# A four-layer graph network on one core: where GpSimd copies the next sixteen gather indices

## The reference, cut to what matters

```python
h = jnp.maximum(_layernorm(x, axis=-1), 0.0)
weight = jnp.einsum('rb,bio->rio', w_comp, bases)     # 32 relations from 8 bases
h_rel = jnp.einsum('ni,rio->rno', h, weight)
msg = h_rel[edge_type_32, src] * edge_weight1
x = x + jax.ops.segment_sum(msg, dst, num_segments=1250) + h_bias
```

## Time and profile before

| | |
|---|---|
| median of 3 runs | 1577.9 us (1575.59 to 1578.49) |
| the profiled execution | 1579.06 us |
| its span in the profile | 1577.2 us |
| TensorE busy in the span | 1462.6 us (93%) |
| VectorE | 993.9 us (63%) |
| ScalarE | 328.9 us (21%) |
| GpSimd | 887.9 us (56%) |
| mean granted TensorE clock | 0.985 of full speed |
| gathers of the first stage (L740) | 36.1 to 449 us of the span |

### The profile page before, as it was taken

The page is one execution under the profiler, slowest core; times in us unless marked ns, Lnnn a source line. Parts: engine busy times, 40 slices in busy tenths (PEclk is TensorE's granted clock), DMA queues, the critical chain, the costliest instruction groups (busy, mean ns, idle before and its releaser), DMA issues.

```text
span 1577.2 us, 24690 instructions
## 1 busy us (share of the span) xinstructions
PE 1462.6 (93%) x6784; PEld 941.4 (60%) x6785; DVE 993.9 (63%) x2781; ACT 328.9 (21%) x806; POOL 887.9 (56%) x932
## 2 busy tenths in 40 slices
PE   4888888888889999999999998999999988999999
PEld 2777777777754444433447576666666655566465
DVE  8766666666666888898633333888888873421111
ACT  7000000000000000000062223555555545411100
POOL 5677777777722777677667761777777760000000
PEclk9999999999999999999999998999999998999999
DMA  4676666776765223422411111322222230000000
GB/s 159 192 198 199 192 203 201 203 202 199 200 173 164 78 74 92 136 83 70 125 61 25 26 28 62 105 72 64 72 65 70 68 54 1 28 0 1 27 34 34
DMA packets 91857, 159.19 MB, mean 101 GB/s; under 512 B 18747, under 2 KB 46960, under 8 KB 91792
## 3 DMA queue, kind: packets, MB, share of 16 engines
q0 software_dynamic: 42832, 103.15, 23.3%
q1 hardware_dynamic: 33728, 29.73, 6.0%
q10 hardware_dynamic: 15232, 25.52, 5.4%
HBM read 140.63 MB, written 17.70 MB: 100 GB/s over the span
## 4 chain that ended last, share of the span: by engine, by line
PE 52%; issue 15%; POOL 14%; DMA 12%; DVE 3%; ACT 1%; POOLq 1%; SPq 1%; DVEq 0%; ACTq 0%
PE ps L1148 14%; PE ps L935 12%; POOL u L801 11%; DMA gath<-h_rows,idx 10%; PE ps L923 9%; PE ps L878 8%; PE ps L1110 4%; POOL gath L740 3%; DMA u<-u_rows,at 2%; PE ps L1129 2%; PE ps L914 1%; PE ps L973 1%; DVE et L1299 0%; PE ps L1085 0%; DMA wc_blk<-in_w_comp_dram 0%
## 5 line engine op out<-in xcount | busy, mean ns | idle before, releaser
L878 PE MATMUL ps<-spread,gath 128*128 128x128 f32 x2504 | 354.9, 290 | 55.1 <-DMA gath<-h_rows,idx 43.8
L766 POOL DMA_INDIRECT slots<-att,idx_s x313 | 313.0, 1000 | 117.2 <-issue 92.9
L878 PEld LDWEIGHTS ps<-spread,gath 128*128 128x128 f32 x2504 | 306.5, 195 | 103.3 <-issue 59.5
L740 POOL DMA_INDIRECT gath<-h_rows,idx x313 | 300.3, 960 | 109.5 <-issue 58.8
L1148 PE MATMUL ps<-base_t,z 128*128 128x512 f32 (+1 forms) x640 | 311.6, 613 | 1.8 <-ACT z L527 1.0
L801 POOL DMA_INDIRECT u<-u_rows,at x243 | 239.1, 984 | 109.7 <-issue 70.7
L1361 DVE TENSOR_TENSOR z<-z,ps 128x512 f32 x313 | 215.0, 687 | 84.1 <-PE ps L878 69.1
L935 PE MATMUL ps<-hs,adj 128*128 128x512 f32 (+3 forms) x400 | 165.5, 414 | 0.0
L1038 PE MATMUL ps<-msg,hot 128*128 128x256 f32 x648 | 158.0, 388 | 6.4 <-DVE msg L1716 5.4
L935 PE MATMUL ps<-hl,adj 128*128 128x512 f32 (+3 forms) x400 | 157.6, 394 | 0.0
L1038 PEld LDWEIGHTS ps<-msg,hot 128*128 128x128 f32 x648 | 120.8, 192 | 56.5 <-DVE msg L1716 36.2
(11 more groups left out here) (264 smaller groups left out, 1678.3 us busy)
## 6 DMA issues: line engine op xcount, KB each, us to landing
base_t<-in_bases_dram ACTq DMA_DIRECT2D x64, 256.0 KB, 2.7
slots<-zero_t SPq DMA_DIRECT2D x6, 896.0 KB, 6.0
at<-slots SPq DMA_DIRECT2D x21, 256.0 KB
att<-in_attr_dram SPq DMA_DIRECT2D x79, 64.0 KB
gath<-h_rows,idx POOLq DMA_INDIRECT x313, 3.7
slots<-att,idx_s POOLq DMA_INDIRECT x313
u<-u_rows,at POOLq DMA_INDIRECT x243, 2.5
z<-in_x_dram SPq DMA_DIRECT2D x9, 256.0 KB, 5.1
```

The costliest lines, as they stand in the source:

```text
L740: nc.gpsimd.indirect_dma_start(out=gath[:, c % RING, :], out_offset=None, in_=h_rows, in_offset=bass.IndirectOffsetOnAxis(ap=idx[:, par, c ...
L766: nc.gpsimd.indirect_dma_start(out=slots, out_offset=bass.IndirectOffsetOnAxis(ap=idx_s[0:r, turn_of, at_quad * QUAD + c:at_quad * QUAD + ...
L878: last = mm(bank[:, k * P:(k + 1) * P], gath[:, h_slot, k * P:(k + 1) * P], s_of.rearrange("p b d -> p (b d)"), start=True, stop=True)
```

## The change

The copy of a lap's indices is no longer the first instruction of the lap. It is issued in the middle of the lap before, between the wait for the slot of gather c = 8 and that gather, into the other half of idx. The copy for the first lap is issued by itself ahead of all gathers. The wait for idx_ok at c = 0 stays, with the same numbers, and so does the count of copies: the last lap of nine gathers issues none. No other engine's program is changed.

```diff
+            def copy_indices(at_chunk, par):
+                nc.gpsimd.tensor_copy(idx[:, par, :], src_i[:, bass.ds(at_chunk, 2 * RING)]).then_inc(idx_ok, 1)
+
             def gather_lap(i, par, first, chunks=2 * RING):
 
                 at_chunk = i * 4 * RING + par * 2 * RING
-                nc.gpsimd.tensor_copy(idx[:, par, :], src_i[:, bass.ds(at_chunk, 2 * RING)]).then_inc(idx_ok, 1)
                 indexed = in_reg(pool, i * 2 + par + 1)
...
                     if c == 0:
                         pool.wait_ge(idx_ok, indexed)
+                    if c == RING and chunks == 2 * RING:
+                        copy_indices(at_chunk + 2 * RING, 1 - par)
                     nc.gpsimd.indirect_dma_start(
...
             with pool.If(pool.value_load(fits[0:1, 0:1], min_val=0, max_val=1) == 1):
+                copy_indices(0, 0)
                 for par in range(2):
                     gather_lap(0, par, par == 0)
```

## The result

| | before | after |
|---|---|---|
| median | 1576.9 us of 4 runs | 1563.5 us of 4 runs (1560.84 to 1566.55) |
| ratio to before | | 0.9907, 95% interval 0.9892 to 0.9923 |
| profiled execution, span | 1579.06, 1577.2 us | 1560.84, 1559.0 us |
| first start of the first to the last gather | 411.95 us | 395.90 us |
| TensorE's mean granted clock | 0.985 | 0.987 |

The kernel is faster by 13.4 us, 0.9%. The forecast was 1574.2 us, and its range ended at 1567: the sign was right, the saving was three to four times what I had put down.

The account below looks back on a forecast made before the run. GpSimd's gathers, one per 1.25 us, were taken to bound the first stage. A gross saving of 10.1 us less 6.4 given back to holds made 3.7, so 1577.9 - 3.7 = 1574.2 us, range 1567 to 1580.

Parts of the forecast that it names:

- TensorE doesn't become the bound: First stage: TensorE has 18.24 us to do in a lap of at least 20.2; its becoming the bound got no chance.
- The hold itself: A gather starting just behind VectorE's spread (L1352) takes longer, by about 0.57 us less the distance between the starts.
- the row that feeds itself: Slower rival, first stage: held gathers sustain themselves, 42 of 75 spreads at 0.43 us, 1582.4 us; chance 0.12.
- the copy's cost behind it: Mid-lap copy: next gather 0.24 us after it, 0.46 from gather to gather, so 0.18 us added a lap.
- the bounds given, 0 to 0.68: Mid-lap copy's cost: 0 if it fits into the 0.30 us between gathers, at most the whole 0.68 of the boundary.
- the gross saving: 19 lap boundaries: 0.71 us removed less 0.18 added by the mid-lap copy, 10.1 us in all.
- the entries: Gathers c = 11 newly caught behind their spread: 5 to 8 of 16, taken as 0.4 of 19 laps.
- The give-back: New holds of gathers by spreads, 9.9 us, less 3.5 us of present extra that goes: 6.4 us net.
- The stall: A gap of 2.19 us between gathers just behind one boundary; a possible further 1.9 us saved, not counted.
- the holds don't grow: Rival: the copy hides in the 0.30 us or the spread comes later; full saving of 10.1 us, 1567.8; chance 0.20.
- The two rivals with more holds: Holds eat the whole saving, 1579.1 us, chance 0.20; or held gathers sustain themselves, 1582.4 us, chance 0.12.
- a gather behind any copy needs 0.78 us: Rival: the gap behind the copy stays, wait or not, so the change saves nothing, 1577.9 us; chance 0.03.

Follow-up runs that it names:

- wait_behind: Changed kernel, but gather c = 8 waits at once for the mid-lap copy ahead of it; 1578.1 us, ratio to the kernel before 0.9996.
- copies2: Changed kernel with the mid-lap index copy cut into two parts, one behind the other; 1575.2 us, ratio to the kernel before 0.9976.
- copies4: Changed kernel with the mid-lap index copy cut into four parts, one behind the other; 1576.8 us, ratio to the kernel before 0.9991.
- copies8_c: Changed kernel with the mid-lap index copy cut into eight parts, one behind the other; 1579.5 us, ratio to the kernel before 1.0008.
- copy_at_15_c: Changed kernel with the next lap's copy between gathers c = 14 and c = 15; 1566.4 us, ratio to the kernel before 0.9919.
- after_again: The changed kernel run once more, unedited; 1566.7 us, ratio to the kernel before 0.9929.

## Why the prediction fell short, point by point

**What held.** GpSimd sets the stage's pace with 1.25 us a gather, and the boundary costs 0.71 us because the queue runs empty behind the wait: the lap fell from 20.72 to 20.11, and wait_behind, which has the copy in its new place and the wait, gave nothing. That TensorE doesn't become the bound held too: 18.24 us of work in 20.11. There are 20 copies, 19 of them between gathers, and no gap of 0.98. The hold itself, a gather caught just behind a spread, with the 0.57 less the distance, is what copies2, copies4 and copies8_c show; the row that feeds itself stands in copy_at_15_c. Two readings of rows were slightly off and bear on nothing: the gap of 0.30 us stands before 289 gathers, not 291, and the four of the earlier trace rows are not the last of the 14 long ones, two come behind them.

**The step that failed** is the copy's cost behind it: "I expect a gather 0.30 - 0.06 = 0.24 us after the copy". Measured is 0.16. The 0.06 came from a copy behind a memset, which isn't a gather behind a copy; the bounds given, 0 to 0.68, were sound, the value taken between them wasn't. It sits in two terms:

- the gross saving: the displacement is 0.10 instead of 0.18 us, so 19 x 0.61 = 11.6 instead of 10.1 us, an error of 1.5;
- the entries: "those less than 0.14 ahead fall behind it by over 0.05 and are held: 5 of 16 ... I take 0.4". With 0.10 us of displacement the edge is at 0.05 ahead, not 0.13, and one of 18 was caught (two in after_again); at copies2's 0.20 it was 13 of 18. The give-back was forecast as 9.9 - 3.5 = 6.4 us; measured is 1.13 - 3.57 = -2.4, so this term is off by 8.8 us, most of the whole error of 10.7 (after_again, with 2.18, would make it 7.8). For the displacement that I put in, its working came near the sum in copies2, with the share of caught laps too low and their cost too high; but it goes from one caught lap to thirteen with 0.1 us more, and I put in one value where the bounds of the gap left it open by several tenths.

**The stall.** "I don't count it, since one profile doesn't say that it recurs." The silence recurs at the same chunk in each of the eleven traces, and the change hides it: 1.9 us. (The gap itself was recorded once, as there is one trace of the kernel before, and again as 1.55 us in copy_at_15_c.) The same sentence of the forecast had said that it begins just behind a boundary with the queue empty, which was the reason to count it.

**The rivals.** What came about is the first, that the holds don't grow, to which I gave 0.20. Its own time, 1567.8, was still too high: 1.5 us for the smaller displacement, 2.4 for the holds that went, 1.9 for the stall make 1562.0, against 1563.5 measured. The two rivals with more holds describe kernels that were not this one: in copies4 the holds and the copies eat nearly all (2.3 us below before), and copy_at_15_c has the row that sustains itself, once. That a gather behind any copy needs 0.78 us fell with the first timeline.

**The range** began at 1567 because I let its lower end be the gross saving with no change in the holds. It should have reached to the same with the present holds and the stall gone: 1577.9 - 13.1 - 3.5 - 1.9 = 1559.4, all numbers that the prediction had.

## What to carry to other kernels

A wait on the engine's own small instruction, put right behind it on the queue that issues gathers, empties that queue, and costs several times the instruction (0.71 us for 0.20): issue the small instruction a few gathers ahead, where the wait is over before it is reached and a lead is left for stalls like the one at chunk 112. Before pricing it, see that this engine sets the pace; where GpSimd waited 2.3 us for a slot every seven to nine gathers, no variant was faster. And where two engines hold each other by the order of starts, the cost of a displacement isn't proportional to it: work out from the trace how many starts lie within the uncertainty of the displacement, and let the range reach to both ends of that.

## What the runs showed of the hardware that I had not expected

- A gather starts 0.16 us after a small copy ahead of it, while it starts 0.30 us after a gather; each further small copy adds about 0.11 us (eight in 1.01 us).
- A VectorE instruction with one SBUF input holds a gather or not by its form: the tensor_scalar (128x512 float32, 0.43 us) does, until 0.12 us before its recorded end, as the two-input one of 0.69 us does; the add from PSUM (0.69 us) doesn't, in 871 gathers beside it.
- The hold is one-sided: a gather loses up to 0.52 us (1.47 in copies2), while no spread of 0.69 us took over 0.79 in any of the traces at this pace, though most start while a gather runs.
- The cost of holds isn't monotone in the displacement: 1.1, 11.8, 8.8 and 0.9 us of extra for 1, 2, 4 and 8 copies.
- GpSimd's sequencer is silent for 3.1 us at two places of the stage, at about the same chunks in nine kernels (eleven traces). With gathers handed over (after: three behind the one that runs) nothing of it is seen, with an empty queue it costs 1.9 us. Its cause is open and wasn't tried.
